# A graph network kernel with runtime window numbers: TensorE loads 16 of them at once in the counts and 24 at once in the attention, instead of 8

## The reference, cut to what matters

```python
msgs = feature[edge_src]
neigh = jax.ops.segment_sum(msgs, edge_dst, num_segments=N_NODES)      # layer 0: 100,000 edges, 6,250 nodes
...
scores = jnp.einsum('ehd,ehd->eh', q[src], k[tgt]) / np.sqrt(HEAD_DIM)  # layer 1: attention
scores = scores + edges @ We + be
...
w = jnp.exp(scores - seg_max[tgt])
...
gathered = edge_val[:, None] * x[edge_col]                              # layer 3: weighted
agg = jax.ops.segment_sum(gathered, edge_row, num_segments=N_NODES)
return agg @ W + b
```

## Time and profile before

| | |
|---|---|
| median of 3 runs | 6285.45 us (6275.57 to 6294.4) |
| profiled execution | 6270.86 us, its span 6268.7 us, granted clock 0.779 |
| busy: PE, PEld, DVE, ACT, POOL | 4219.9, 2834.4, 3516.1, 1951.6, 2395.1 us |
| counts stage | 571 to 1329 us of the span |
| attention with the building of the weights | 1836 to 5109 us |
| chain that ended last | PE at_p3t L1604 8% (the last layer), the page follows it no further back |

### The profile page before, as it was taken

One profiled execution on the slowest core, in us unless ns is written; L12 is line 12 of the kernel. 1 busy time (PEld: TensorE's weight loads), 2 busy tenths in 40 slices (PEclk: granted clock), 3 DMA queues, 4 the chain that ended last, 5 costly groups with the idle time before them and its releaser, 6 DMA issues. The chain is left out here.

```text
span 6268.7 us, 91469 instructions
## 1 busy us (share of the span) xinstructions
PE 4219.9 (67%) x26649; PEld 2834.4 (45%) x26650; DVE 3516.1 (56%) x4701; ACT 1951.6 (31%) x3223; POOL 2395.1 (38%) x2303
## 2 busy tenths in 40 slices
PE   3556654549955666666666666666666653799999
PEld 2324332339932333333333333333333332798888
DVE  3313889876654655565655555655555565774000
ACT  2334243556630011112222222333333333664000
POOL 3320179023324544455444444444444423431000
PEclk7777555559976777777877788778787765899999
DMA  7535563336642223333333334434444442567887
GB/s 128 156 122 173 131 226 118 154 155 223 218 136 51 73 80 88 93 103 103 111 108 110 113 113 122 130 117 122 130 123 127 132 165 88 185 223 249 295 300 266
DMA packets 595115, 918.46 MB, mean 147 GB/s; under 512 B 107581, under 2 KB 519571, under 8 KB 575502
## 3 DMA queue, kind: packets, MB, share of 16 engines
q1 hardware_dynamic: 413600, 527.25, 26.0%
q10 hardware_dynamic: 117359, 250.68, 10.9%
q0 software_dynamic: 64032, 139.15, 9.1%
HBM read 611.74 MB, written 314.96 MB: 148 GB/s over the span
## 5 line engine op out<-in xcount | busy, mean ns | idle before, releaser
L2005 POOL DMA_INDIRECT at_qg<-q_d,at_slot x1616 | 1574.0, 974 | 1666.1 <-DVE at_S L2132 1180.4
L997 PE MATMUL bw_ps<-bw_mov,bw_sta 128*128 128x392 bf16 x7056 | 1815.1, 373 | 556.0 <-issue 514.0
L997 PEld LDWEIGHTS bw_ps<-bw_mov,bw_sta 128*128 128x128 bf16 x7056 | 666.0, 106 | 1081.2 <-issue 867.6
L2048 PE MATMUL at_psk<-at_kp,at_hot 128*128 x4848 | 672.5, 244 | 624.6 <-DVE at_qg L2126 305.8
L2048 PEld LDWEIGHTS at_psk<-at_kp,at_hot 128*128 128x128 bf16 x4848 | 463.4, 106 | 1032.9 <-issue 859.7
L2126 DVE TENSOR_TENSOR at_qg<-at_qg,at_psk 128x816 f32<-128x816 f32 (+1 forms) x303 | 274.1, 905 | 1159.0 <-DMA et_dist<-in_edge_weight 1014.3
L1019 ACT COPY xall<-bw_ps 128x392 f32<-128x392 f32 x520 | 252.3, 485 | 1442.6 <-PE bw_ps L997 707.2
L902 PE MATMUL ba_ps<-ba_mov,ba_sta 128*128 128x196 bf16 x2368 | 440.2, 352 | 329.2 <-issue 203.4
L838 DVE TENSOR_TENSOR bw_mov<-bw_ps,late_lo 128x3136 bf16<-128x3136 f16 x294 | 523.7, 1781 | 145.1 <-PE bw_ps L997 72.5
L981 DVE TENSOR_TENSOR bw_sta<-bw_raw,late_kw 128x1024 bf16<-128x1024 bf16 x882 | 554.4, 682 | 0.0
L1604 PE MATMUL at_p3t<-tile,room 128*128 128x256 f32 (+1 forms) x2450 | 525.1, 376 | 4.9 <-ACT room L1166 4.9
(11 more groups left out here) (545 smaller groups left out, 5115.6 us busy)
## 6 DMA issues: line engine op xcount, KB each, us to landing
tile<-adw_d SPq DMA_DIRECT2D x23, 6272.0 KB, 18.7
adw_d<-xall ACTq DMA_DIRECT2D x65, 1568.0 KB
adj_d<-ba_stage ACTq DMA_DIRECT2D x50, 1568.0 KB, 5.2
l0raw<-adj_d SPq DMA_DIRECT2D x50, 1568.0 KB, 6.5
tile<-adj_d SPq DMA_DIRECT2D x50, 1568.0 KB, 6.5
adw_d<-bw_stage ACTq DMA_DIRECT2D x33, 1568.0 KB
at_rel<-rel_d SPq DMA_DIRECT2D x101, 512.0 KB
et_attr<-in_edge_attr SPq DMA_DIRECT2D x48, 1024.0 KB
```

Source lines behind the costliest of these rows:

```text
L997: ins = pe.matmul(self.ps[:, bass.DynSlice(place, WCOL)], self.sta[:, k, u // 2, :, u % 2], self.mov[:, u // 2, :, u % 2], start=False, st ...
L2005: pool.indirect_dma_start(out=qg[:, ring, b, :], out_offset=None, in_=q_d[:, :], in_offset=bass.IndirectOffsetOnAxis(ap=slot[:, ring, b:b ...
L2048: ins = pe.matmul(ps_k[:, at:at + KW], hot[:, par, sum(ROUNDS[:r]) + u, :], kp[:].rearrange("p j k n -> p (j k n)")[:, bass.DynSlice(place ...
```

## The change

The counts load 16 numbers with one instruction and wait for the hots once per 16 visits; the attention loads all 24 numbers of a group at its start, and the loads of the second and third third are gone. Executed loads of window numbers go from 296 to 148 in the counts and from 294 to 98 in the attention, each writing 16 and 24 registers in place of 8. Nothing else is changed; the arithmetic is the same.

```diff
@@ CountBuild.registers
-        return self.nc.values_load_multi_w_load_instructions(self.c.wreg[0:1, bass.DynSlice(t, UV)], engines=(mybir.EngineType.PE,), ...)[1]
+        return self.nc.values_load_multi_w_load_instructions(self.c.wreg[0:1, bass.DynSlice(t, UC)], engines=(mybir.EngineType.PE,), ...)[1]
@@ WeightBuild.registers
-        return self.nc.values_load_multi_w_load_instructions(self.c.wreg[0:1, bass.DynSlice(t, UV)], engines=(mybir.EngineType.PE,), ...)[1]
+        return self.nc.values_load_multi_w_load_instructions(self.c.wreg[0:1, bass.DynSlice(t, 3 * UV)], engines=(mybir.EngineType.PE,), ...)[1]
@@ build_counts
         with nc.tensor.Fori(0, NVISV // RING) as i:
-            for u0 in range(0, RING, UV):
+            for u0 in range(0, RING, UC):
                 regs = b.registers(i * RING + u0)
-                for u in range(UV):
+                for u in range(UC):
                     b.visit(i * RING + u0 if u == 0 else None, u0 + u, regs[u])
@@ attention
-        def octet(g, third):
-            return build.registers((3 * g + third) * UV)
-
         def visits(g, par, third, us, regs):
             for u in us:
-                build.visit((3 * g + third) * UV if u == 0 else None, slot_of(par, third) + u, regs[u])
+                build.visit((3 * g + third) * UV if u == 0 else None, slot_of(par, third) + u, regs[third * UV + u])
@@ tensor_group
             places = places_of(g, 0)
             if building:
-                regs = octet(g, 0)
+                regs = build.registers(3 * g * UV)
             pe.wait_ge(s_hot, g + 3)
...
             if building:
                 visits(g, par, 0, (6, 7), regs)
-                regs = octet(g, 1)
                 visits(g, par, 1, (0, 1), regs)
...
             if building:
-                regs = octet(g, 2)
                 visits(g, par, 2, (0, 1), regs)
```

More of the change, by code:

```diff
@@ L890, in registers @@
     def registers(self, t):
-        return self.nc.values_load_multi_w_load_instructions(self.c.wreg[0:1, bass.DynSlice(t, UV)], engines=(mybir.EngineType.PE,), min_val=0, max_val=NWV + SLOTS, skip_runtime_bounds_check_because="the table holds window numbers by construction")[1]
+        return self.nc.values_load_multi_w_load_instructions(self.c.wreg[0:1, bass.DynSlice(t, UC)], engines=(mybir.EngineType.PE,), min_val=0, max_val=NWV + SLOTS, skip_runtime_bounds_check_because="the table holds window numbers by construction")[1]
     def visit(self, t, u, reg):
@@ L984, in registers @@
     def registers(self, t):
-        return self.nc.values_load_multi_w_load_instructions(self.c.wreg[0:1, bass.DynSlice(t, UV)], engines=(mybir.EngineType.PE,), min_val=0, max_val=NW + BANKS, skip_runtime_bounds_check_because="the table holds window numbers by construction")[1]
+        return self.nc.values_load_multi_w_load_instructions(self.c.wreg[0:1, bass.DynSlice(t, 3 * UV)], engines=(mybir.EngineType.PE,), min_val=0, max_val=NW + BANKS, skip_runtime_bounds_check_because="the table holds window numbers by construction")[1]
     def visit(self, t, u, reg):
```

## The result

The changed kernel takes 6298.12 us (median of 20 runs), the kernel before 6284.94 in as many; the ratio is 1.0023, with a 95% interval of 1.0015 to 1.0031. The profiled execution took 6298.59 us, its span 6296.4. The counts' half of the change did what the working said and a little more (44 us in the trace); the attention gave all of it back and took more: 13 us by the medians, 28 between the two profiled executions, of which the one of before lay 14 us under its median.

A forecast was written before the change was run, and what follows sets the result against it. PE, at 4.28 us a batch against DVE's 3.97, was taken to bound the counts, and POOL's gathers with what follows them the attention; -38 + 3 = -35 us on the median 6285.45 gave 6250 us, range 6203 to 6285.

The forecast's parts named there:

- Counts: Counts stage: one load boundary per batch instead of two, 3.98 us a batch in place of 4.28, 127 times, -38 us.
- The stores' disturbance: Counts: loads slowed behind stores of `adj_d`, now 75 us; change taken as 0, between -20 and +70.
- The load of 24: Attention, group's start: 16 more registers, +1.12 us before round 0; loads of 1.7 to 2.3 us expected.
- 1.22 us of room: Attention: gap between round 0's last key matmul and DVE taking it, set against the load's +1.12 us.
- rival 3: Attention: the 24-register load is disturbed and overruns DVE's room by 4.4 us; 6317 us, chance 0.08.
- The step that failed: Attention: DVE's lateness is swallowed by its wait for gathers, even 3 us in most groups; +3 us, from -5 to +15.
- rival 2: Counts: gain mostly eaten by more disturbed longer loads or by DVE, level with PE; 6270 to 6300 us, chance 0.23.
- lie under waits: Attention: loads of the second and third thirds are covered by waits, so removal gains nothing; uncovered, worth 169 us.
- What was announced for the attention: Attention profile: POOL's and DVE's waits were to stay within some 10 us of before.

## Why the prediction was wrong

- **Counts: right, a little small.** The load of 16 registers takes 1.109 us (1.15 forecast), the batch 3.95 (3.98), and the stage became 44 us shorter (38). PE's issue idle fell by 86 us where some 40 were announced. The stores' disturbance, taken as neutral, is 1.29 us in the place shown instead of 1.49, which is on the side of the gain. The gain was passed on whole, to the first layer.
- **The load of 24: right in size** (1.79 us in a range of 1.7 to 2.3). Of the 1.2 us more, 0.47 reached round 0 on average. The "1.22 us of room" of DVE's product of round 0 nearly held, too: it started within 0.3 us of the end of round 0 in 7 of the 92 groups before and in 9 now, and the announced start of rival 3, that it would follow directly in most groups, did not come. The room was there; it was round 1 that had none.
- **The step that failed** is "What is late on DVE then still stands ahead of the wait for gathers, so even a delay of 3 us is swallowed there in most groups", with +3 us for the attention; it measured +68, and +47 on another occasion. I had read DVE's 1014.3 us before products, and the 7.85 us before 3334.52, as a wait for gathered rows. It isn't one: the rows of a group are gathered three groups ahead, for the group shown by 3146.09 with its product at 3248.87, and in no group of the two traces less than 93 us before its product of round 1. DVE and PE hardly issue at all in that stretch, on this kind of chip. Such time is no cover for PE's work; what isn't finished when it begins goes on at 0.7 us or a multiple of it an instruction. The trace of before showed it, in 29 groups with a round 1 of over 8 us beside a normal 3.9, and in rows such as the earlier trace rows's 514.0 us of issue idle, and I did not ask what these groups had in common. Why the engines issue so slowly there stays open. That such idle time stands in nearly every group was read rightly (over 2 us before the product of round 1 in 94 of the 101), but not what it is.
- **Rival 3** named the right place and the right end, by another mechanism: it wanted the load of 24 itself disturbed. Its median is 1.791, so it mostly isn't. That 6298 us lies in rival 2's 6270 to 6300 is chance: the counts' gain was not eaten. That the removed loads "lie under waits" held nearly: they were worth 20 us, not 169.
- **What was announced for the attention**, POOL's and DVE's waits within 10 us of before, did not come: they moved by 72 and 110 us, and pointed straight at the attention.

## What to carry to other kernels

Idle time in front of an instruction covers work only if the engine could have worked in it: before counting on a wait, look whether its releaser is really a producer of what the instruction reads, and whether the engines issue anything meanwhile. Work that such a stretch catches can take several times as long (18 us in place of 4 for a round 1 here), though averaged over the groups the cost stayed below the 1.2 us by which the load grew, and an advance of 0.86 us gained nothing. So put loads and waits behind the work that must be over before the stretch. A change worth parts of a per cent has to be measured on the chip it is meant for: here it is 0.991 on one kind and 1.002 on another.

## What the runs showed of the hardware that was not expected

- A register load by TensorE grew about in proportion to its size up to 24: 0.592 us for 8, 1.109 for 16, 1.791 for 24 (medians; the 24 are of the attention's load), 69 to 75 ns a register; ACT took 0.311 at least for 4.
- Chips differ: 4945 and 4973 us against 6281, 6366 and 6367 for the same program. On the second kind, from about the eighth of 16 indirect gathers in a row to some 4 us behind the start of the last, TensorE's matmuls come 0.7 us or a multiple of it apart, 0.8 to 1.4 a us, and VectorE starts 0.2 to 0.3 instructions a us. Why, no run here shows; nor whether it is the chip or something else of the occasion: only one chip came twice, both times of the second kind.
- One and the same chip, by its number, ran the kernel before in 6281 us on one occasion and in 6366 on another, 85 us apart, over six times the 13 us of the result. Only runs of one occasion can be compared at that size.
